# Three of four heads turned in blocks through HBM, cached values loaded in one contiguous transfer

## The chip, the cores and the metric

The kernel runs on one core of a Trainium2 chip. Its five engines are TensorE (PE; PEld are its weight loads), VectorE (DVE), ScalarE (ACT), GpSimd (POOL) and SyncE (SP), which here issues nearly all DMAs. The metric is the device time of one execution in microseconds.

## The reference, cut to what matters

For 8 sequences of 128 tokens and width 512 the reference computes a layer with LoRA and a first attention (32 heads of 16), adds the result to x, then a second attention with grouped heads over a paged cache, then a feed-forward layer with low-rank experts, and adds that too. The change touches the second attention alone:

```python
q = _rope(_rmsnorm(q, q_norm_w), pos)          # 32 query heads of 128
k = _rope(_rmsnorm(k, k_norm_w), pos)          # 8 key heads, 128 new keys
kc = k_cache[block_table].reshape(bsz, L, HK, D)   # 16 pages of 32 keys: L = 512
k_all = jnp.concatenate([kc, k], axis=1)       # 640 keys
v_all = jnp.concatenate([vc, v], axis=1)
scores = jnp.einsum('bqhd,bkhd->bhqk', q, k_all) * SCALE
probs = jax.nn.softmax(jnp.where(valid, scores, -1e+30), axis=-1)
o = jnp.einsum('bhqk,bkhd->bqhd', probs, v_all)
return jnp.einsum('bse,de->bsd', o, Wo)        # summed over all heads
```

## The kernel before, in words

The first stage (`phase1`) ends at about 250 us of the profile. Beside its own work it gathers the cached pages of each sequence into the HBM tensor `kv_of_batch` (`gather_four`, line 86). The second stage (`phase2`) runs 64 items: for each of 8 key heads g the 8 sequences b. An item has four query heads (`REP`). All products are done to nearly full f32 precision by splitting each factor into a rounded high part (`_h`, made on ACT) and a remainder (`_l`, made on DVE or POOL), and three matmuls.

The probabilities of a head come out with the queries on the partitions (`pf`, 128 x 640) and are needed with the keys on the partitions. Two ways do this. Heads in `BY_PE` are turned by five PE transposes into PSUM (line 1317), copied by ACT (`high`, line 1486) and subtracted by DVE (`low`, line 1610). Heads in `BY_DMA` are turned by DVE in blocks of 32 x 32 into `blk` (line 1604), stored to HBM (`blocks_away`, line 1217) and loaded back by four DMAs that put the blocks into their places in `moved` (`blocks_back`, line 1226); ACT then makes the high part (`high_moved`, line 1492) and POOL the remainder (`low_moved`, line 1745). Heads 0 and 1 go by DMA, heads 2 and 3 by PE. `ck` and `cv` hold the cached keys and values of an item.

The order of each engine's work is written out by hand: each engine has a function `slot(m, one, two, last)`, called once per item. In the slot of item m the scores of its heads 1 to 3 are computed, the values of item `last` are multiplied, item `one`, which follows, is made ready and its head 0 started, and queries and keys of item `two` are projected. Engines run their lists strictly in order and meet by semaphores. PE's scores of one head wait for DVE's `minima` (line 1590) of the head before, since both use the same two PSUM banks. ACT's `exponent` (line 1480) follows the minima. In the slots with b equal to 5 and 6 the next head's projection weights are split, on POOL by `q_weights` (line 1697) and `kv_weights` (line 1703); in those with b equal to 0 and 1 the output weights are. `rope_queries` is line 1722, `rope_keys` lines 1728 and 1731, `rms` 1715 and 1717, the remainders of cached keys and values lines 1739 and 1735. SP's `key_rows` (line 1204) waits until POOL has read the keys before (`kcl_sb`), `value_rows` (line 1210) until it has read the values before (`vcl_sb`). The third stage, from about 1252 us, is the feed-forward layer.

## Time and profile before

| | us |
|---|---|
| median of 3 runs | 1304.53 (1304.43 to 1305.79) |
| profiled execution, its own time | 1303.22 |
| its span in the profile | 1301.4 |
| PE busy | 1252.7 |
| DVE busy | 984.4 |
| ACT busy | 835.0 |
| POOL busy | 830.8 |
| DMA queue q1, share of 16 engines' span | 51.0% |

The span is what the profile covers; the execution's own time is 1.8 us longer. Busy times count work, not waiting, and PE's contains overlapping instructions once. Times in the rows below are from the span's start.

### The profile page before, as it was taken

Reading aid. Unit: us, or ns where it says so; the run is one execution under the profiler, and the core shown is the slowest. Engines: PE = TensorE matmul, PEld = TensorE weight load, DVE = VectorE, ACT = ScalarE, POOL = GpSimd, SP = SyncE. Lnnn points to the kernel's source line nnn. Section 1 sums busy time; section 2 is a strip of 40 time slices with the busy share of each in tenths; the row PEclk is TensorE's granted clock in tenths of the full one; section 3 lists DMA queues with packets and bytes.
Section 4 is the critical chain, followed back from the end, with each engine's and each line's share of the span. In section 5 each row is a group of like instructions: output and inputs, shape, how many; then the busy total and the mean of one; then the engine's idle time right before and its main releaser. Section 6 shows DMA issues by size and latency. Waiting matters only on the chain. (4 is left out here: it accounts for less than half of the span.)

```text
span 1301.4 us, 26180 instructions
## 1 busy us (share of the span) xinstructions
PE 1252.7 (96%) x7464; PEld 1067.8 (82%) x7464; DVE 984.4 (76%) x2380; ACT 835.0 (64%) x2501; POOL 830.8 (64%) x783
## 2 busy tenths in 40 slices
PE   5899998799999999999999999999999999999988
PEld 4666765588888888888888888888888888888878
DVE  3577757478878878888788788868888888888866
ACT  2677777466676666666766666666667666666731
POOL 1457557476767676668765876577667756775731
PEclk9899998899999999999999999999999999999999
DMA  8555553445555545555555555545555555555541
GB/s 288 214 200 205 203 211 130 111 117 139 137 139 141 140 133 149 131 140 141 151 130 141 138 140 128 144 126 139 131 140 143 137 142 142 135 138 137 137 130 66
DMA packets 288561, 191.48 MB, mean 147 GB/s; under 512 B 151201, under 2 KB 256674, under 8 KB 287266
## 3 DMA queue, kind: packets, MB, share of 16 engines
q1 hardware_dynamic: 287408, 189.64, 51.0%
q8 instruction: 61, 1.00, 0.3%
q14 instruction: 82, 0.67, 0.2%
q10 hardware_dynamic: 1010, 0.17, 0.1%
HBM read 143.60 MB, written 79.69 MB: 172 GB/s over the span
## 5 line engine op out<-in xcount | busy, mean ns | idle before, releaser
L1745 POOL TENSOR_TENSOR b_p_l<-b_moved,b_p_h 128x640 fp32r<-128x640 f32 x128 | 200.9, 1570 | 167.4 <-PE ps L1341 86.5
L1480 ACT ACTIVATE b_pf<-b_sm,b_mn 128x640 f32<-128x640 f32 x256 | 212.2, 829 | 128.0 <-DVE b_mn L1590 127.9
L1590 DVE CUSTOM_DVE_ANT_0 b_sm<-ps,mask_row,b_rstd 128x640 f32<-128x640 f32 x256 | 224.9, 878 | 51.8 <-PE ps L1267 46.5
L1492 ACT ACTIVATE b_p_h<-b_moved 128x640 fp32r<-128x640 f32 x128 | 94.6, 739 | 163.5 <-DMA b_moved<-blocks_of_probs 162.0
L1626 DVE SCALAR_TENSOR_TENSOR b_hacc<-ps,b_ri,b_hacc 128x512 f32<-128x512 f32 x248 | 182.4, 736 | 4.3 <-PE ps L1267 4.0
L1265 PE MATMUL ps<-b_w_h,x1t_h 128*128 128x512 f32 (+1 forms) x512 | 179.3, 350 | 0.1
L1265 PE MATMUL ps<-b_kt_h,b_qt_h 128*128 128x320 f32 x512 | 168.9, 330 | 6.0 <-DVE b_mn L1590 5.7
L1266 PE MATMUL ps<-b_w_l,x1t_h 128*128 128x512 f32 (+1 forms) x512 | 173.8, 340 | 0.0
L1267 PE MATMUL ps<-b_w_h,x1t_l 128*128 128x512 f32 (+1 forms) x512 | 173.6, 339 | 0.0
L1267 PE MATMUL ps<-b_kt_h,b_qt_l 128*128 128x320 f32 x512 | 158.9, 310 | 0.0
L1266 PE MATMUL ps<-b_kt_l,b_qt_h 128*128 128x320 f32 x512 | 158.7, 310 | 0.0
L1610 DVE TENSOR_TENSOR b_p_l<-ps,b_p_h 128x640 fp32r<-128x640 f32 x128 | 104.8, 819 | 41.1 <-ACT b_p_h L1486 41.1
L1604 DVE STREAM_TRANSPOSE b_blk<-b_pf 128x640 f32<-128x640 f32 x128 | 107.7, 842 | 35.2 <-ACT b_pf L1480 34.3
L1735 POOL TENSOR_TENSOR b_v_l<-b_cv,b_v_h 128x512 fp32r<-128x512 f32 x64 | 82.9, 1295 | 58.8 <-ACT b_v_h L1462 58.8
L711 POOL TENSOR_TENSOR a_pr<-a_pr,a_ri 128x512 f32<-128x512 f32 x64 | 68.4, 1078 | 74.8 <-DVE a_ri L586 74.8
L1265 PEld LDWEIGHTS ps<-b_kt_h,b_qt_h 128*128 128x128 f32 x512 | 96.8, 189 | 14.5 <-DVE b_mn L1590 8.1
L1267 PEld LDWEIGHTS ps<-b_w_h,x1t_l 128*128 128x128 f32 x512 | 96.7, 189 | 12.0
L431 ACT ACTIVATE a_pr<-a_sm,a_mn 128x128 f32<-128x128 f32 x256 | 99.0, 396 | 10.9 <-PE ps L304 10.6
L1265 PEld LDWEIGHTS ps<-b_w_h,x1t_h 128*128 128x128 f32 x512 | 97.0, 189 | 9.7 <-issue 0.8
L1265 PE MATMUL ps<-b_wo_h,b_o_h 128*128 128x512 f32 x256 | 101.6, 397 | 3.1 <-DVE b_o_l L1614 2.0
L1266 PEld LDWEIGHTS ps<-b_w_l,x1t_h 128*128 128x128 f32 x512 | 97.1, 190 | 8.7
L1333 PE MATMUL ps<-b_p_h,b_v_l 128*128 128x512 f32 x256 | 102.4, 400 | 0.0
(170 smaller groups left out, 3344.6 us busy)
## 6 DMA issues: line engine op xcount, KB each, us to landing
blocks_of_probs<-b_blk SPq DMA_DIRECT2D x128, 320.0 KB, 2.5
b_moved<-blocks_of_probs SPq DMA_DIRECT2D x512, 80.0 KB, 2.0
kv_of_batch<-in_kv SPq DMA_DIRECT2D x128, 256.0 KB
b_ck<-kv_of_batch SPq DMA_DIRECT2D x64, 256.0 KB, 4.0
b_cv<-kv_of_batch SPq DMA_DIRECT2D x256, 64.0 KB, 1.9
raw<-in_w SPq DMA_DIRECT2D x32, 384.0 KB, 3.2
raw<-in_wo SPq DMA_DIRECT2D x32, 256.0 KB, 2.8
a_xt<-in_xt SPq DMA_DIRECT2D x8, 256.0 KB, 5.6
```

The source lines that it names most:

```text
L431: op = act.activation(pr[:, c % 4, j], sm[:, c % 2, j], ACT.Exp, bias=mn[:, h:h + 1], scale=-1.0, accum_out=rs[:, h:h + 1])
L1265: pe.matmul(out, lhs[0], rhs[0], start=start, stop=False)
L1266: pe.matmul(out, lhs[0], rhs[1], start=False, stop=False)
L1267: return pe.matmul(out, lhs[1], rhs[0], start=False, stop=stop)
L1333: mm = pe.matmul(ps[:, OT, :], l, p_h[:, i], start=False, stop=False)
L1480: act.activation(pf[:, h % 2], sm[:, h % 2], ACT.Exp, bias=mn[:, m.b % 2, h:h + 1], scale=-1.0, accum_out=rs[:, m.b % 2, h:h + 1]).then_in ...
L1492: act.activation(blocks_of(p_h[:, :, h * P:(h + 1) * P]), moved[:, d].rearrange("p (a t j) -> p a t j", a=LT, j=QUAD), ACT.Copy).then_inc( ...
L1590: dve.tensor_tensor_reduce(sm[:, h % 2], score_row, mask_row[:, m.b], rstd[:, m.b % 4, h:h + 1], -MASKED, ALU.add, ALU.min, mn[:, m.b % 2, ...
L1604: dve.transpose(by_quadrant(blk[:, d]), by_tile(pf[:, h % 2])).then_inc(blk_sb, 1)
L1610: dve.tensor_tensor(p_l[:, :, cols], turned_row, p_h[:, :, cols], ALU.subtract).then_inc(pl_sb, 1)
L1626: dve.scalar_tensor_tensor(out=hacc[:, m.b], in0=ps[:, OUT[h], :], scalar=share, in1=hacc[:, m.b], op0=ALU.mult, op1=ALU.add).then_inc(h_s ...
L1745: pool.tensor_tensor(blocks_of(p_l[:, :, h * P:(h + 1) * P]), moved[:, d].rearrange("p (a t j) -> p a t j", a=LT, j=QUAD), blocks_of(p_h[: ...
```

## The change

Head 2 moves from `BY_PE` to `BY_DMA`. `blk` and `moved` keep two rooms, so heads 0 and 2 share one, and new waits order them. Head 2's copy on ACT and its subtraction on POOL are placed in the following slot. ACT's copy of head 0 moves behind the exponent of head 3. `kv_of_batch` holds keys and values apart, and the values of an item are loaded by one DMA that gives each partition four keys in a row (2 KB). Partition p of tile t thus holds key 4p + t instead of 128t + p, and so the probabilities of cached keys are read with a step of four elements, by DVE's block transposes (which become two instructions, since the 128 new keys keep their order) and by PE's transposes.

```diff
...
 LAST = B - 1
-BY_DMA = (0, 1)
-BY_PE = (2, 3)
+BY_DMA = (0, 1, 2)
+BY_PE = (3,)
+ROOMS = 2
 QUAD = 32
...
         n = first + k
-        sp.dma_start(kv_dram[n // NPP, :, n % NPP], t["kv"][bass.ds(four[k], 1)].rearrange("a g n -> (a g) n")).then_inc(gathered, 16)
+        page = t["kv"][bass.ds(four[k], 1)].rearrange("a g (k n) -> (a g) k n", k=2)
+        sp.dma_start(kv_dram[n // NPP, :, :, n % NPP], page).then_inc(gathered, 16)
 
...
         hacc = sb("hacc", [P, B, D])
-        blk = sb("blk", [P, len(BY_DMA), NK])
-        moved = sb("moved", [P, len(BY_DMA), NK])
+        blk = sb("blk", [P, ROOMS, NK])
+        moved = sb("moved", [P, ROOMS, NK])
 
...
 
+        def last_in_room(d):
+            return max(e for e in range(len(BY_DMA)) if e % ROOMS == d % ROOMS)
+
         def by_quadrant(ap):
...
         def by_tile(ap):
-            return ap.rearrange("p (t c j) -> p c t j", c=LT, j=QUAD)
+            return ap.rearrange("p (c j t) -> p c t j", c=LT, j=QUAD)
+
+        def by_rows(ap):
+            return ap.rearrange("p (c j) -> p c j", j=QUAD)
 
...
                 wait(sp, kcl_sb, m.n)
-                keys = kv_dram[m.b, m.g, :, 0:HD * PSIZE].rearrange("j (d s) -> d j s", d=HD)
+                keys = kv_dram[m.b, m.g, 0].rearrange("j (d s) -> d j s", d=HD)
                 sp.dma_start(ck[:].rearrange("p (j s) -> p j s", s=PSIZE), keys).then_inc(ck_in, 16)
...
                 wait(sp, vcl_sb, m.n)
-                for q in range(LT):
-                    rows_of = kv_dram[m.b, m.g, :, HD * PSIZE:].rearrange("(t q) (s d) -> q s t d", q=LT, d=HD)[q]
-                    sp.dma_start(cv[q * PSIZE:(q + 1) * PSIZE], rows_of).then_inc(cv_in, 16)
+                rows_of = kv_dram[m.b, m.g, 1].rearrange("j (p n) -> (j p) n", n=LT * HD)
+                sp.dma_start(cv[:].rearrange("p t d -> p (t d)"), rows_of).then_inc(cv_in, 16)
 
...
                 wait(sp, moved_in[d], 16 * LT * m.n)
-                sp.dma_start(blocks_dram[d], blk[:, d]).then_inc(blk_out[d], 16)
+                sp.dma_start(blocks_dram[d], blk[:, d % ROOMS]).then_inc(blk_out[d], 16)
 
...
                 sp.wait_ge(blk_out[d], 16 * (m.n + 1))
-                wait(sp, ml_sb, len(BY_DMA) * (m.n - 1) + d + 1)
+                wait(sp, ml_sb, len(BY_DMA) * m.n + d + 1 - ROOMS if d >= ROOMS else len(BY_DMA) * (m.n - 1) + last_in_room(d) + 1)
                 for c in range(LT):
                     rows_of = blocks_dram[d].rearrange("(a i) (c n) -> c i a n", a=LT, c=LT)[c]
-                    sp.dma_start(moved[c * QUAD:(c + 1) * QUAD, d].rearrange("p (a n) -> p a n", a=LT), rows_of).then_inc(moved_in[d], 16)
+                    sp.dma_start(moved[c * QUAD:(c + 1) * QUAD, d % ROOMS].rearrange("p (a n) -> p a n", a=LT), rows_of).then_inc(moved_in[d], 16)
 
...
                 blocks_back(m, 1)
+                blocks_away(m, 2)
+                blocks_back(m, 2)
                 if two:
...
                 for i in range(NT):
-                    mm = pe.transpose(turned_row[:, i], pf[:, h % 2, i * P:(i + 1) * P], ident[:])
+                    keys = pf[:, h % 2, L:] if i == LT else pf[:, h % 2, i:L:LT]
+                    mm = pe.transpose(turned_row[:, i], keys, ident[:])
                 mm.then_inc(pt_ps, 1)
...
                     turn_new(one)
-                turn_probs(m, 2)
                 if two:
...
             def cache_values(m):
-                act.wait_ge(cv_in, 16 * LT * (m.n + 1))
+                act.wait_ge(cv_in, 16 * (m.n + 1))
                 wait(act, pv_ps, m.n - 1)
...
                 wait(act, pvh_ps, m.n)
-                act.activation(blocks_of(p_h[:, :, h * P:(h + 1) * P]), moved[:, d].rearrange("p (a t j) -> p a t j", a=LT, j=QUAD),
+                act.activation(blocks_of(p_h[:, :, h * P:(h + 1) * P]), moved[:, d % ROOMS].rearrange("p (a t j) -> p a t j", a=LT, j=QUAD),
                                ACT.Copy).then_inc(mh_sb, 1)
...
                     high(last, 3)
+                    high_moved(last, 2)
                 exponent(m, 1)
...
                     kv_weights(m.g + 1)
-                high_moved(m, 0)
                 if last:
...
                 exponent(m, 3)
-                high(m, 2)
+                high_moved(m, 0)
                 if one:
...
             high(end, 3)
+            high_moved(end, 2)
             h_out(act, 2)
...
                 dve.wait_ge(exp_sb, REP * m.n + h + 1)
-                wait(dve, blk_out[d], 16 * m.n)
-                dve.transpose(by_quadrant(blk[:, d]), by_tile(pf[:, h % 2])).then_inc(blk_sb, 1)
+                wait(dve, blk_out[d - ROOMS], 16 * (m.n + 1)) if d >= ROOMS else wait(dve, blk_out[last_in_room(d)], 16 * m.n)
+                blocks = by_quadrant(blk[:, d % ROOMS])
+                dve.transpose(blocks[:, :, 0:LT], by_tile(pf[:, h % 2, 0:L]))
+                dve.transpose(blocks[:, :, LT], by_rows(pf[:, h % 2, L:])).then_inc(blk_sb, 1)
 
...
                 minima(m, 3)
+                turn_blocks(m, 2)
                 if last:
...
                     invert(last)
-                low(m, 2)
                 if one:
...
                 wait(pool, pv_ps, m.n)
-                pool.tensor_tensor(blocks_of(p_l[:, :, h * P:(h + 1) * P]), moved[:, d].rearrange("p (a t j) -> p a t j", a=LT, j=QUAD),
+                pool.tensor_tensor(blocks_of(p_l[:, :, h * P:(h + 1) * P]), moved[:, d % ROOMS].rearrange("p (a t j) -> p a t j", a=LT, j=QUAD),
                                    blocks_of(p_h[:, :, h * P:(h + 1) * P]), ALU.subtract).then_inc(ml_sb, 1)
...
                     rms(one)
+                if last:
+                    low_moved(last, 2)
+                if one:
                     rope_keys(one)
...
             slots(pool, slot)
+            low_moved(end, 2)
             pool_ffn(pool)
...
     x1_dram = nc.dram_tensor("x1", [B, S, D], F32).ap()
-    kv_dram = nc.dram_tensor("kv_of_batch", [B, G, NPP, 2 * HD * PSIZE], F32).ap()
+    kv_dram = nc.dram_tensor("kv_of_batch", [B, G, 2, NPP, HD * PSIZE], F32).ap()
     with ExitStack() as ctx:
```

The first place is POOL, from the queries' rope in the slot with b = 5 to the cached keys' remainder in that with b = 6. `b_rstd` is rms, `b_ka` the keys' rope, `b_w_l` weights, `b_kt_l` the cached keys' remainder. Before:

```order
L1722 TENSOR_TENSOR b_ra<-b_ra,b_rb 128x512 [waits b_qab_sb]
L1697 TENSOR_TENSOR b_w_l<-raw,b_w_h 128x512 [waits b_wqh_sb] x2
L1715 TENSOR_SCALAR b_rstd<-b_ss 128x5 [waits b_ksq_sb,b_exp_sb]
L1717 TENSOR_TENSOR b_rstd<-b_rstd,half 128x5 [waits b_ms_sb]
L1728 TENSOR_TENSOR b_ka<-b_ka,b_kb 128x128 [waits b_rstd_sb,b_kab_sb]
L1731 TENSOR_SCALAR b_ka<-b_ka,b_rstd 128x128 [waits b_kab2_sb]
L1697 TENSOR_TENSOR b_w_l<-raw,b_w_h 128x512 [waits b_wqh_sb] x2
L1739 TENSOR_TENSOR b_kt_l<-b_ck,b_kt_h 128x512 [waits b_kch_sb]
```

and now:

```order
L1734 TENSOR_TENSOR b_ra<-b_ra,b_rb 128x512 [waits b_qab_sb]
L1709 TENSOR_TENSOR b_w_l<-raw,b_w_h 128x512 [waits b_wqh_sb] x2
L1727 TENSOR_SCALAR b_rstd<-b_ss 128x5 [waits b_ksq_sb,b_exp_sb]
L1729 TENSOR_TENSOR b_rstd<-b_rstd,half 128x5 [waits b_ms_sb]
L1757 TENSOR_TENSOR b_p_l<-b_moved,b_p_h 128x4x5x32 [waits b_pv_ps,b_mh_sb]
L1740 TENSOR_TENSOR b_ka<-b_ka,b_kb 128x128 [waits b_rstd_sb,b_kab_sb]
L1743 TENSOR_SCALAR b_ka<-b_ka,b_rstd 128x128 [waits b_kab2_sb]
L1709 TENSOR_TENSOR b_w_l<-raw,b_w_h 128x512 [waits b_wqh_sb] x2
L1751 TENSOR_TENSOR b_kt_l<-b_ck,b_kt_h 128x512 [waits b_kch_sb]
```

One more subtraction of moved blocks, that of head 2 of the item before, stands between rms and the keys' rope; after it the order is as before.

The second place is SP in an ordinary slot, from the first block store to the values. `blocks_of_probs<-b_blk` is a store, `b_moved<-blocks_of_probs` the loads, `b_ck` keys and `b_cv` values. Before:

```order
L1217 DMA blocks_of_probs<-b_blk 128x640 [waits b_moved_in0,b_blk_sb]
L1226 DMA b_moved<-blocks_of_probs 32x4x160 [waits b_ml_sb,b_blk_out0]
L1226 DMA b_moved<-blocks_of_probs 32x4x160 x3
L1217 DMA blocks_of_probs<-b_blk 128x640 [waits b_moved_in1,b_blk_sb]
L1204 DMA b_ck<-kv_of_batch 128x16x32 [waits b_kcl_sb]
L1226 DMA b_moved<-blocks_of_probs 32x4x160 [waits b_ml_sb,b_blk_out1]
L1226 DMA b_moved<-blocks_of_probs 32x4x160 x3
L1210 DMA b_cv<-kv_of_batch 32x4x128 [waits b_vcl_sb]
L1210 DMA b_cv<-kv_of_batch 32x4x128 x3
```

and now:

```order
L1224 DMA blocks_of_probs<-b_blk 128x640 [waits b_moved_in0,b_blk_sb]
L1233 DMA b_moved<-blocks_of_probs 32x4x160 [waits b_ml_sb,b_blk_out0]
L1233 DMA b_moved<-blocks_of_probs 32x4x160 x3
L1224 DMA blocks_of_probs<-b_blk 128x640 [waits b_moved_in1,b_blk_sb]
L1212 DMA b_ck<-kv_of_batch 128x16x32 [waits b_kcl_sb]
L1233 DMA b_moved<-blocks_of_probs 32x4x160 [waits b_ml_sb,b_blk_out1]
L1233 DMA b_moved<-blocks_of_probs 32x4x160 x3
L1224 DMA blocks_of_probs<-b_blk 128x640 [waits b_moved_in2,b_blk_sb]
L1233 DMA b_moved<-blocks_of_probs 32x4x160 [waits b_ml_sb,b_blk_out2]
L1233 DMA b_moved<-blocks_of_probs 32x4x160 x3
L1217 DMA b_cv<-kv_of_batch 128x512 [waits b_vcl_sb]
```

A store and four loads for head 2 stand ahead of the values, which are one DMA instead of four.

## Rows read from the trace of the kernel before

**Rows 1.** The page's first part: busy us (share of the span) xinstructions.

```profile
PE 1252.7 (96%) x7464; PEld 1067.8 (82%) x7464; DVE 984.4 (76%) x2380; ACT 835.0 (64%) x2501; POOL 830.8 (64%) x783
```

**Rows 2.** Busy by stretch: us, PE, PEld, DVE, ACT, POOL; clock, DMA share, GB/s.

```profile
250.00:1252.00 1002.00, 992.62 (x5667) 871.13 (x5667) 799.39 (x1579) 669.12 (x1834) 688.93 (x639) 0.99 0.52 137
673.20:688.90 15.70, 15.70 (x94) 13.84 (x92) 12.72 (x26) 9.91 (x29) 9.07 (x9) 1.00 0.58 148
720.20:735.90 15.70, 15.70 (x94) 13.84 (x91) 12.59 (x25) 10.46 (x23) 14.59 (x13) 1.00 0.44 121
735.90:751.50 15.60, 14.96 (x83) 12.63 (x82) 11.44 (x23) 11.15 (x37) 10.96 (x11) 1.00 0.56 147
```

**Rows 3.** PE in order of time: start, us, line, op, tiles, count.

```profile
681.37 0.71 PE L1317 MATMUL ps<-ident,b_pf 128*128 128x128 f32 x5
681.83 0.48 PE L1265 MATMUL ps<-b_w_h,x1t_h 128*128 128x512 f32 x1
682.15 0.39 PE L1266 MATMUL ps<-b_w_l,x1t_h 128*128 128x512 f32 x1
682.38 0.39 PE L1267 MATMUL ps<-b_w_h,x1t_l 128*128 128x512 f32 x1
```

**Rows 4.** DVE in order of time, the same slot.

```profile
676.17 0.28 DVE L1571 TENSOR_TENSOR b_ka<-ps,cw 128x128 f32<-128x128 f32 x1
676.37 0.28 DVE L1573 TENSOR_TENSOR b_kb<-ps,sw 128x128 f32<-128x128 f32 x1
...
678.10 0.84 DVE L1604 STREAM_TRANSPOSE b_blk<-b_pf 128x640 f32<-128x640 f32 x1
...
683.50 0.83 DVE L1610 TENSOR_TENSOR b_p_l<-ps,b_p_h 128x640 fp32r<-128x640 f32 x1 [0.63 <-ACT b_p_h L1486]
```

**Rows 5.** Groups, 440:1240: busy us, mean ns | idle before.

```profile
L1492 ACT ACTIVATE b_p_h<-b_moved 128x640 fp32r<-128x640 f32 x102 | 75.4, 739 | 128.4 <-DMA b_moved<-blocks_of_probs 126.9 <-PE ps L1333 1.4
...
L1745 POOL TENSOR_TENSOR b_p_l<-b_moved,b_p_h 128x640 fp32r<-128x640 f32 x102 | 160.2, 1570 | 124.8 <-PE ps L1341 70.6 <-ACT b_p_h L1492 54.1
```

**Rows 6.** DMA issues: count, KB each, us from issue to landing.

```profile
blocks_of_probs<-b_blk SPq DMA_DIRECT2D x128, 320.0 KB, 2.5
b_moved<-blocks_of_probs SPq DMA_DIRECT2D x512, 80.0 KB, 2.0
```

**Rows 7.** SP in order of time, an ordinary slot and the seventh.

```profile
681.93 1.91 SPq L1226 DMA_DIRECT2D b_moved<-blocks_of_probs  x4
...
730.14 0.38 SPq L1204 DMA_DIRECT2D b_ck<-kv_of_batch  x1
730.62 2.59 SPq L1226 DMA_DIRECT2D b_moved<-blocks_of_probs  x4
```

**Rows 8.** ACT in order of time, two slots [idle before].

```profile
675.43 0.83 ACT L1480 ACTIVATE b_pf<-b_sm,b_mn 128x640 f32<-128x640 f32 x1 [0.91 <-DVE b_mn L1590]
...
689.48 0.70 ACT L1486 ACTIVATE b_p_h<-ps 128x640 fp32r<-128x640 f32 x1
...
735.30 0.74 ACT L1492 ACTIVATE b_p_h<-b_moved 128x640 fp32r<-128x640 f32 x1 [4.18 <-DMA b_moved<-blocks_of_probs]
```

**Rows 9.** POOL in order of time, first and last of ten instructions.

```profile
719.60 1.30 POOL L1722 TENSOR_TENSOR b_ra<-b_ra,b_rb 128x512 f32<-128x512 f32 x1
...
728.81 1.30 POOL L1739 TENSOR_TENSOR b_kt_l<-b_ck,b_kt_h 128x512 fp32r<-128x512 f32 x1
```

**Rows 10.** DVE's block transposes: an ordinary one (689.20), three late ones.

```profile
360.41 0.84 DVE L1604 STREAM_TRANSPOSE b_blk<-b_pf 128x640 f32<-128x640 f32 x1 [1.56 <-ACT b_pf L1480]
...
689.20 0.84 DVE L1604 STREAM_TRANSPOSE b_blk<-b_pf 128x640 f32<-128x640 f32 x1 [0.33 <-ACT b_pf L1480]
...
737.91 0.85 DVE L1604 STREAM_TRANSPOSE b_blk<-b_pf 128x640 f32<-128x640 f32 x1 [2.05 <-ACT b_pf L1480]
...
1118.12 0.85 DVE L1604 STREAM_TRANSPOSE b_blk<-b_pf 128x640 f32<-128x640 f32 x1 [1.24 <-ACT b_pf L1480]
```

**Rows 11.** PE in order of time, after the seventh slot.

```profile
738.99 0.66 PE L1293 MATMUL ps<-ident,b_ra 128*128 128x128 f32 x4 [0.64 <-POOL b_ra L1722]
```

## The prediction

> **What bounds the kernel now.** I read the page's busy times, then the busy times by stretch, then each engine in order of time. [Rows 1] show TensorE (PE) busy for 96% of the span. [Rows 2] cut the second stage, 250 to 1252 us, out of it: 992.6 of 1002.0 us are PE time, at a granted clock of 0.99. The stage has 64 items, so an item takes 1002.0 / 64 = 15.66 us, and the slots of one head (eight items) show PE 15.70 of 15.70 us while DVE has 12.7, ACT 10 to 11 and POOL 9.07 in an ordinary slot but 14.59 in the seventh, where the next head's weights are split. Only after that seventh slot does PE lose time: 14.96 of 15.60 us. So in seven slots of eight a matmul taken away is time taken away, as long as nothing else becomes late; around the seventh slot something else ends last.
>
> **What the change takes from PE.** One of two groups of five turns per item goes (head 2). [Rows 3] show the group start at 681.37 us and the next matmul at 681.83 us, 0.46 us; that matmul's successor comes 0.32 us later where the following pairs are 0.23 us apart, so 0.09 us more belong to the group. 64 x 0.55 = 35.2 us.
>
> **What it adds, off PE.** On DVE, the remainder of head 2 (0.83 us at 683.50, with 0.63 us of waiting for ACT ahead of it) goes and a third block transpose comes (0.84 us at 678.10) [rows 4]. Each block transpose is now two instructions, 512 and 128 elements wide. Small instructions of 128 elements stand 0.20 us apart [rows 4]; the small one can cost from nearly nothing beyond its share of the work (0.20 less a fifth of 0.84, so 0.03 us) to the whole 0.20 us. I take 0.1 us, 0.3 per item. DVE then has 12.7 - 0.83 + 0.84 + 0.3 = 13.0 of 15.1 us. The new transpose follows the minima of head 3, which themselves follow the exponent of head 2 by their order, so it waits for nothing. ACT exchanges one copy of 640 columns for another, of 739 ns [rows 5]: nothing, with some 5 us of idle time per item. POOL gets a third 1570 ns subtraction [rows 5]: 9.1 + 1.6 = 10.7 of 15.1 us, free in an ordinary slot.
>
> On the queue, SP gets one store and four loads more and three loads of values fewer. Four loads take SP 1.91 us (at 681.93), and landings take 2.5 and 2.0 us [rows 6, 7]. For head 2: the last load of head 1 is issued by 683.84 us, then 2.5 us until the store has landed, 1.9 us of issuing and 2.0 us of landing: 690.2 us. The copy that wants it stands behind ACT's copy of head 3, which ends at 690.18 us [rows 8], 0.55 us earlier once the slot is shorter. So it is some 0.6 us late, and what waits behind it on ACT is the exponent of head 1, which already stood idle 0.91 us for DVE [rows 8] and so hides it; if landings grow by 1 us, this cover is gone, and the exponent delays the minima of head 3 on DVE. The values' load moves behind the loads of head 2, which wait for POOL's subtraction of head 0. It is wanted only in the next slot (a slot of 15 us against some 5 us of delay), so nothing. DMA queues are busy for 0.52 of the stage [rows 2]; 640 KB more per item on some 2.1 MB make it 0.65 at most, less what 2 KB rows for the values save. The cache gather writes the same bytes in two pieces per row: nothing, under the first stage.
>
> **The seventh slot.** Here POOL works without a gap: the queries' rope, two weights, rms, the keys' rope, two weights and the cached keys' remainder run from 719.60 to 730.11 us, ten instructions [rows 9]. SP's load of keys waits for that last one and starts at 730.14; the loads of head 1's blocks stand behind it, at 730.62 [rows 7]. ACT stood idle 4.18 us for them and took them at 735.30 [rows 8]; the exponent behind them was late, and so was DVE's block transpose at 737.91, with 2.05 us of idle time where an ordinary slot has 0.33 [rows 10]. The minima that free the score banks for PE follow it. POOL's own last piece, the queries' rope, held PE for 0.64 us at 738.99 [rows 11]. The late block transpose stands at the end of seven heads (the first at 360.41, the last at 1118.12). The change puts head 2's subtraction, 1.57 us, into this chain, ahead of the keys' rope. The chain begins in the sixth slot (where POOL takes up 719.60) and ends in the eighth, so the two groups of turns that PE saves inside it, 1.1 us, are not gained either. Its price is between 0 (if its slack were as large as it) and 7 x (1.57 + 1.1) = 18.7 us; since PE waited here already, I take all of it.
>
> **The sum.** 1303.2 (the profiled execution) - 35.2 + 18.7 = 1286.7 us. The median of the runs is 1.3 us above that execution: 1288.
>
> **A price that no row shows: strided reads.** DVE and PE now read the probabilities of cached keys with a step of four elements, 16 bytes; every read of that tile so far was contiguous. Below, it is nothing, and a gain is excluded, since the same elements are read. Above, I double the strided part: on DVE 0.84 x 512/640 = 0.67 us per transpose, 2.0 us per item; on PE four of five turns at 0.46 / 5 = 0.093 us, 0.37 us per item. I take nothing, which is what [rows 3, 4] show for the contiguous form, and keep the other end as a rival.
> The Trainium skill speaks against it: SBUF — State Buffer, Specifications (TRN2), says that SBUF delivers lines of 16 bytes and that full bandwidth needs at least two reads in each. By that rule each read here would open a new line, and the time would be that of rival 1 below; by [rows 3, 4] it would be the sum above. No run so far shows it.
>
> **The rivals.**
> 1. *Strided reads are charged.* DVE gets 13.0 + 2.0 = 15.0 us of work per item plus the waits that its order can't lose, 0.33 us for the exponent [rows 10] and about as much for the scores: 15.7 to 15.8 us; DVE then paces, from an extra cost of about 0.45 us per transpose on. With the seventh slots' chain (7 x 1.6 us, and 7 x 1 us as the transposes in it grow), 1303 + 64 x 0.12 + 18 + 1.3 = 1330. Nothing in the trace speaks for or against it, since no instruction of this stage reads such a step. That is slower than before.
>    The page named above, of the Trainium skill, is what makes me hold this for possible.
> 2. *POOL's chain has room.* If the subtraction slips in where POOL would wait anyway, all 35 us are gained: 1303.2 - 35.2 + 1.3 = 1269. Against it: ten instructions in 10.5 us of [rows 9].
> 3. *The third head comes back late.* If the extra transfers lengthen the landings by 1 us, ACT's in-order copy of head 2 holds the exponent of head 1 for some 0.6 us per item more than it idled, and the loads of head 0 on SP wait for POOL's subtraction of head 2. Half of that reaching PE gives 0.3 x 56 = 17 us: 1305. For it: ACT's 4.18 us for such loads in [rows 8]; against: the 0.91 us of idle time there.
> 4. *Only one of the two engines is charged* for the strides: PE alone, at half of its 0.37 us per item, 64 x 0.2 = 13 us more than the forecast: 1301.
>
> **Chances.** Forecast 0.42, rival 1 0.27, rival 2 0.12, rival 3 0.12, rival 4 0.07. A measurement of this kernel tells 0.2% (2.6 us) from no change. Faster: nearly all of the forecast and rival 2, about half of rivals 3 and 4, together 0.60; within 0.2%: 0.07; slower: rival 1 and the rest, 0.33. The forecast's own range is 1276 to 1297: 12 us less if two thirds of the chain's price are hidden, 9 more if half as much again comes on top. For 8 in 10 it reaches from 1268 down at rival 2 to 1328, just short of rival 1's middle.
>
> **What the profile after will show.** Right: 320 turns on PE, slots of 15.1 us in the first five of a head, block transposes of about 0.7 and 0.2 us, a PE wait of some 2 to 4 us after each seventh slot, released by DVE's minima. Wrong: block transposes of 1.2 us or more, a pitch of turns above 0.1 us, ordinary slots with PE waiting for minima (rival 1); or ACT's copy of head 2 idle for over 1.5 us in ordinary slots (rival 3).

## The result: 4.7% slower

The changed kernel takes **1363.51 us** (median, 1362.68 to 1364.49), the kernel before beside it 1304.48 (1297.11 to 1305.79). The ratio is 1.0469, interval 1.0441 to 1.0498. The forecast of 1288 us was wrong in sign, and the time lies outside its own range (1276 to 1297) and above the wider one (1268 to 1328). The profiled execution has a span of 1360.9 us, 59.5 us more than that of before (1301.4).

The page's first part and the busy times by stretch of the kernel after answer to [rows 1, 2]:

```profile
PE 1251.9 (92%) x7144; PEld 1043.4 (77%) x7144; DVE 1057.9 (78%) x2572; ACT 828.5 (61%) x2501; POOL 925.0 (68%) x847
```
```profile
250.00:1310.00 1060.00, 992.98 (x5347) 848.14 (x5345) 870.11 (x1765) 661.73 (x1834) 779.25 (x699) 0.98 0.61 168
```

TensorE has 320 matmuls fewer. The stage is 58 us longer, and by these rows the growth is idle time of TensorE: 67 us now, 9 before. But its busy time should have fallen by some 31 us and didn't, so part of it is slower work; that is taken up below. No other engine is near full. The slots show where the time sits. I measure a slot from one group of turns of head 3 to the next, in TensorE's order of time; this is the second full head of each kernel (us; the last column but one is the next head's first slot):

```
slot of sequence      2      3      4      5      6      7      8      1      sum
before              15.66  15.66  15.66  15.66  15.66  15.66  16.19  15.66  125.8
after               15.80  19.04  15.18  15.17  15.55  17.14  19.15  15.17  132.2
```

An undisturbed slot did become shorter, 15.17 instead of 15.66 us, as forecast (15.1). In most heads two or three of eight are undisturbed; the others are not. Over the stage the mean slot of after is (1313.35 - 259.63) / 63 = 16.73 us.

A slot in which TensorE stands idle long can cost twice. Here is the eighth slot of that head and four of its microseconds (us, PE, PEld, DVE, ACT, POOL; granted clock, DMA share, GB/s):

```profile
494.29:513.44 19.15, 17.17 (x88) 14.43 (x86) 13.45 (x29) 11.81 (x38) 13.21 (x12) 0.91 0.60 166
497.00:498.00 1.00, 0.33 (x2) 0.00 (x0) 0.17 (x1) 1.00 (x5) 1.00 (x2) 1.00 0.64 172
498.00:499.00 1.00, 0.11 (x1) 0.11 (x2) 1.00 (x2) 0.82 (x3) 0.91 (x2) 1.00 0.83 168
501.00:502.00 1.00, 1.00 (x5) 0.81 (x4) 1.00 (x3) 0.86 (x2) 1.00 (x2) 0.50 0.41 161
502.00:503.00 1.00, 1.00 (x4) 0.81 (x3) 1.00 (x3) 0.27 (x1) 0.83 (x2) 0.50 0.03 8
```

From 497 to 500 us TensorE was busy for 1.02 us (0.58 in the third microsecond). From 501 to 504 its granted clock was 0.50, that is 1.2 instead of 2.4 GHz, and from 505 on full again. So this slot has 2.0 us of idle time and 2.0 us more of busy time than an undisturbed one. Ten of the 63 slots of after show a mean clock of 0.91 or 0.92; before has one, the slot of 19.65 us in its fifth head. From the eight whole ones (busy 137.7 us, where the other long slots have 15.4 to 16.0 each) I estimate that the lower clock makes 12 to 16 of the 59 us. It is a consequence of the waiting, and adds to it.

The queue at fault, as the experiments below bear out, belongs to none of the busy engines: it is that of SyncE (SP), which issues all transfers in order and waits in between. Here is its order of time in after for one slot (start, us of issuing), answering to [rows 7]. L1224 is the store of a head's blocks, L1233 the four loads back, L1212 keys, L1217 values:

```profile
813.38 1.73 SPq L1233 DMA_DIRECT2D b_moved<-blocks_of_probs  x4
815.15 0.43 SPq L1217 DMA_DIRECT2D b_cv<-kv_of_batch  x1
816.56 0.44 SPq L1224 DMA_DIRECT2D blocks_of_probs<-b_blk  x1
820.52 1.74 SPq L1233 DMA_DIRECT2D b_moved<-blocks_of_probs  x4
822.36 0.38 SPq L1224 DMA_DIRECT2D blocks_of_probs<-b_blk  x1
822.94 0.38 SPq L1212 DMA_DIRECT2D b_ck<-kv_of_batch  x1
825.06 1.74 SPq L1233 DMA_DIRECT2D b_moved<-blocks_of_probs  x4
826.90 0.38 SPq L1224 DMA_DIRECT2D blocks_of_probs<-b_blk  x1
829.23 1.73 SPq L1233 DMA_DIRECT2D b_moved<-blocks_of_probs  x4
```

Read it as three trips (heads 0, 1, 2): store, wait until it has landed, four loads. From head 2's loads at 813.38 to the next at 829.23 it is 15.85 us, more than the 15.17 that TensorE needs. SP's own waits between 440 and 1250 us, summed, say what stands behind whom (us, times, longest); L63 is the helper that waits, here for GpSimd's subtractions. After, and then two lines of before:

```profile
SPq L1233 <- DMA blocks_of_probs<-b_blk: 186.7, 116, 4.1
SPq L63 <- POOL b_p_l L1757: 151.4, 66, 4.0
SPq L1224 <- DVE b_blk L1616: 29.6, 43, 1.6
SPq L1212 <- POOL b_kt_l L1751: 17.4, 13, 2.7
```
```profile
SPq L1226 <- DMA blocks_of_probs<-b_blk: 177.5, 97, 3.1
SPq L1217 <- DVE b_blk L1604: 115.0, 87, 6.7
```

SP waits for blocks from VectorE only 29.6 us in 810, where it was 115.0 before: now it is nearly always late. ScalarE, in order of time, is where the lateness enters the computation, answering to [rows 8]; L1501 is a copy of a head that came back, L1489 an exponent:

```profile
812.62 0.74 ACT L1501 ACTIVATE b_p_h<-b_moved 128x640 fp32r<-128x640 f32 x1 [3.13 <-DMA b_moved<-blocks_of_probs]
...
814.26 0.85 ACT L1489 ACTIVATE b_pf<-b_sm,b_mn 128x640 f32<-128x640 f32 x1
...
818.05 0.74 ACT L1501 ACTIVATE b_p_h<-b_moved 128x640 fp32r<-128x640 f32 x1 [1.83 <-DMA b_moved<-blocks_of_probs]
818.69 0.81 ACT L1489 ACTIVATE b_pf<-b_sm,b_mn 128x640 f32<-128x640 f32 x1
```

Each exponent starts with no wait of its own, right behind the copies: what held it is the copy ahead of it. The exponent feeds VectorE's block transpose, whose blocks SP stores: a ring of two in-order queues. GpSimd stands in a second ring: its subtraction of head 2 ended at 820.44 (818.86 + 1.58), and head 0's loads, which need the same room, start at 820.52:

```profile
818.86 1.58 POOL L1757 TENSOR_TENSOR b_p_l<-b_moved,b_p_h 128x640 fp32r<-128x640 f32 x1 [1.05 <-ACT b_p_h L1501]
```

TensorE itself names only the last link, VectorE's minima and GpSimd's rotary products (PE waits, 250 to 1310 us), as [rows 11] did:

```profile
PE ps L1274 <- DVE b_mn L1600: 31.7, 44, 2.4
PE ps L1302 <- POOL b_ra L1734: 26.4, 23, 2.8
PE ps L1342 <- ACT b_p_h L1501: 5.6, 8, 1.1
```

The two terms that the prediction left open, as groups of VectorE and TensorE's weight loads (count, busy us, mean ns), and the landings, answering to [rows 3, 4, 6]:

```profile
L1615 DVE STREAM_TRANSPOSE b_blk<-b_pf 128x512 f32<-128x512 f32 x192 | 214.1, 1115 | 109.2 <-ACT b_pf L1489 105.2 <-DMA blocks_of_probs<-b_blk 4.0
L1616 DVE STREAM_TRANSPOSE b_blk<-b_pf 128x128 f32<-128x128 f32 x192 | 52.3, 272 | 0.0
```
```profile
713.14 0.76 PE L1327 MATMUL ps<-ident,b_pf 128*128 128x128 f32 x5
713.66 0.39 PE L1274 MATMUL ps<-b_kt_h,b_qt_h 128*128 128x320 f32 x1
```
```profile
blocks_of_probs<-b_blk SPq DMA_DIRECT2D x192, 320.0 KB, 2.7
b_moved<-blocks_of_probs SPq DMA_DIRECT2D x768, 80.0 KB, 2.0
```

### The profile page after: what moved, and what is told of

It reads as the page before. It is cut to its first block and busy times, and to the rows that moved or that the text cites. A ratio compares the mean times of both kernels' runs of the same rounds, so it can differ in the third digit from the quotient of the medians.

```text
span 1360.9 us, 26051 instructions
## 1 busy us (share of the span) xinstructions
PE 1251.9 (92%) x7144; PEld 1043.4 (77%) x7144; DVE 1057.9 (78%) x2572; ACT 828.5 (61%) x2501; POOL 925.0 (68%) x847
## 5 line engine op out<-in xcount | busy, mean ns | idle before, releaser
L1757 POOL TENSOR_TENSOR b_p_l<-b_moved,b_p_h 128x640 fp32r<-128x640 f32 x192 | 301.7, 1571 | 262.6 <-ACT b_p_h L1501 262.1
L1615 DVE STREAM_TRANSPOSE b_blk<-b_pf 128x512 f32<-128x512 f32 x192 | 214.1, 1115 | 109.2 <-ACT b_pf L1489 105.2
L1501 ACT ACTIVATE b_p_h<-b_moved 128x640 fp32r<-128x640 f32 x192 | 141.7, 738 | 220.9 <-DMA b_moved<-blocks_of_probs 220.6
L1489 ACT ACTIVATE b_pf<-b_sm,b_mn 128x640 f32<-128x640 f32 x256 | 212.0, 828 | 51.8 <-DVE b_mn L1600 51.1
L1274 PE MATMUL ps<-b_kt_h,b_qt_h 128*128 128x320 f32 x512 | 171.9, 336 | 32.5 <-DVE b_mn L1600 31.7
L1507 ACT ACTIVATE b_o_h<-ps 128x512 fp32r<-128x512 f32 x64 | 38.3, 599 | 128.9 <-PE ps L1351 128.9
L1342 PE MATMUL ps<-b_p_h,b_v_h 128*128 128x512 f32 x256 | 108.3, 423 | 5.6 <-ACT b_p_h L1501 5.6
L1343 PE MATMUL ps<-b_p_h,b_v_l 128*128 128x512 f32 x256 | 107.3, 419 | 0.0
```

The costliest lines, as they stand in the source:

```text
L1274: pe.matmul(out, lhs[0], rhs[0], start=start, stop=False)
L1342: pe.matmul(ps[:, OT, :], h, p_h[:, i], start=i == 0, stop=False)
L1343: mm = pe.matmul(ps[:, OT, :], l, p_h[:, i], start=False, stop=False)
L1489: act.activation(pf[:, h % 2], sm[:, h % 2], ACT.Exp, bias=mn[:, m.b % 2, h:h + 1], scale=-1.0, accum_out=rs[:, m.b % 2, h:h + 1]).then_in ...
L1501: act.activation(blocks_of(p_h[:, :, h * P:(h + 1) * P]), moved[:, d % ROOMS].rearrange("p (a t j) -> p a t j", a=LT, j=QUAD), ACT.Copy).t ...
L1615: dve.transpose(blocks[:, :, 0:LT], by_tile(pf[:, h % 2, 0:L]))
```

## The experiments

Times are medians; runs of one group shared a chip and its runs of the kernel before (1306.18, 1304.88, 1305.62, 1303.31 and 1303.39 us in the order of the groups; 1303.67 for the last run, whose runs of before were its own).

### First group: which part, and which suspect

**Three heads alone** (values loaded as before, no strided reads):

```diff
-rows_of = kv_dram[m.b, m.g, 1].rearrange("j (p n) -> (j p) n", n=LT * HD)
-sp.dma_start(cv[:]...)
+for q in range(LT):
+    sp.dma_start(cv[q * PSIZE:(q + 1) * PSIZE], rows_of).then_inc(cv_in, 16)
...
-dve.transpose(blocks[:, :, 0:LT], ...)   # 512, step 4
-dve.transpose(blocks[:, :, LT], ...)     # 128
+dve.transpose(blocks, by_tile(pf[:, h % 2]))   # 640, contiguous
...
-keys = pf[:, h % 2, L:] if i == LT else pf[:, h % 2, i:L:LT]
+keys = pf[:, h % 2, i * P:(i + 1) * P]         # TensorE's turns
```


> Three heads by DMA as after, but values loaded as before (four DMAs, keys 128t + p), so that no read has a step of 16 bytes and each block transpose is one instruction. Theory A (DVE's strided transposes, 1115 ns for 512 columns where the 128-column one takes 272, set the pace): DVE loses 3 x 0.54 us per item and the time falls to 1285 to 1300. Theory B (SP's one queue, three store-landing-load trips in a row per item, sets the pace): three more DMAs on SP, so 1355 to 1375, about that of after.

Measured 1425.69 us (1423.99 to 1426.74), ratio 1.0900 [1.0862, 1.0939]: slower still by 62 us. So the strides are not the cause, and the value load was worth something after all: the four value loads take SP 2.02 us to issue where one takes 0.43. An extra 1.6 us of SP's time costs about 1 us a slot, and SP waits for blocks from VectorE 0.7 us in all (440 to 1250 us): SP paces. Part of the 62 us is again the clock: 21 slots are below 0.93, where after has ten. Undisturbed slots take 15.10 to 15.12 us, so all of the 0.55 us that the prediction wanted from TensorE is there once the reads are contiguous.

```profile
816.85 2.02 SPq L1218 DMA_DIRECT2D b_cv<-kv_of_batch  x4
```

**The value layout alone** (two heads by DMA, one value load, strided reads):

```diff
-BY_DMA = (0, 1, 2)
-BY_PE = (3,)
+BY_DMA = (0, 1)
+BY_PE = (2, 3)
```


> Two heads by DMA as before, with the new layout of values: one DMA of 2 KB rows, strided reads by DVE (two transposes) and by PE (ten turns). Theory A: DVE gets 2 x 0.54 us per item more and the time rises to 1325 or more. Theory B: SP's queue is shorter than before; only PE's turns, if they take longer, and the seventh slots show: 1300 to 1312.

Measured 1317.04 (1314.61 to 1325.84), ratio 1.0080 [1.0053, 1.0107]. Its undisturbed slots are 15.75 us against 15.66: two groups of strided turns, 0.05 us each by that, 0.06 by the order of time of after (0.52 us from 713.14 to 713.66, against 0.46 in [rows 3]). That makes 6 us; the rest stands in the eighth slots, 123.1 us for seven of them against 116.1 in before (its trace is of the longest of its seven runs, 1325.84 us). The two parts don't add: +11 and +120 alone, +59 together. The layout costs a little where TensorE paces and pays where SP does.

**A room for each head** in the tile that the loads fill:

```diff
-moved = sb("moved", [P, ROOMS, NK])
+moved = sb("moved", [P, len(BY_DMA), NK])
...
+wait(sp, ml_sb, len(BY_DMA) * (m.n - 1) + d + 1)   # each head waits for its own subtraction only
```


> After, with a room of its own in moved for each of the three heads (blk keeps two), so SP's loads of head 0 don't wait for POOL's subtraction of head 2, nor those of head 2 for head 0's. If the shared room is what holds SP (the profile names POOL for 161 us of SP's waits), 1335 to 1350; if it is the landings of the stores (198 us of SP's waits) or DVE, 1360 to 1365.

Measured 1362.52 (1355.4 to 1369.15), ratio 1.0414 [1.0355, 1.0473]: no gain that can be told from none. SP's wait for GpSimd is gone, but its wait for landings rose from 186.7 to 313.7 us. Cutting the ring through GpSimd only uncovers the other.

**No round trip for head 2** (its store and loads are left out, and its blocks are read where they lie, in a room of their own, so its probabilities stand in wrong places; with that the wait of head 0's loads for GpSimd's subtraction of head 2 goes too):

```diff
-blocks_away(m, 2)
-blocks_back(m, 2)
```


> After, without head 2's store and loads: ACT and POOL read head 2 straight from DVE's blocks, whose places are then wrong, all other work is as after. Theory B: SP's chain and 640 KB per item go, 1290 to 1310 (POOL's seventh slot and DVE's strides stay). Theory A: 1350 or more, since DVE's work is unchanged.

Measured 1317.43 (1316.29 to 1320.22), ratio 1.0086 [1.0050, 1.0122]: head 2's trip is 46 of the 59 us, the shared room included, which by itself was worth nothing in the run before. But with no trip at all the kernel is still 11 us slower than before, in slots at the heads' boundary (its eighth slots take 17.6 to 20.7 us).

### Second group: order, bytes, queue, stride

**Other loads into SP's wait** for head 2's store:

```diff
 blocks_away(m, 2)
-blocks_back(m, 2)
 if two: value_rows(two)
 ...                     # weight chunks
+blocks_back(m, 2)
```


> The changed kernel with only the order of SyncE's queue edited: the value load and the weight chunks of a slot are issued between head 2's store and its four loads back, where SyncE otherwise waits for the store to land. Same bytes, same instructions. Theory S (SyncE's one in-order queue sets the long slots: three times store, wait for the landing, four loads): these issues, 0.43 us for the values and 0.43 us for a chunk, leave the chain, up to 0.9 us of each long slot, and the next head 0's store no longer lands behind them; about 35 of the 64 slots are long, so 20 to 40 us come back: 1325 to 1345 us. Theory D (the 640 KB more of DMA traffic per item make every landing late): the traffic is the same, 1358 to 1368.

Measured 1383.44 (1381.31 to 1386.61), ratio 1.0596 [1.0570, 1.0623]: theory S, as I put it, missed by 40 us and in sign. SP's waiting for landings did fall (186.7 to 85.6 us), but the value load now waits for GpSimd ahead of head 2's loads (62.2 us), and ScalarE's waits for loads grew from 171.9 to 210.5 us. My reading is that what counts is when head 2 comes back, not how long SP waits.

**A quarter of head 2's bytes**, every issue and wait kept (three quarters of its rows are not moved):

```diff
+rows = slice(0, QUAD) if h == 2 else slice(0, P)
-sp.dma_start(blocks_dram[d], blk[:, d % ROOMS])
+sp.dma_start(blocks_dram[d, rows], blk[rows, d % ROOMS])
...
+if h == 2: room, rows_of = room[:, 0:1], rows_of[:, 0:1]   # each of the four loads
```


> The changed kernel with every DMA of head 2's trip kept in its place, but each moving only a quarter of its rows (32 of 128 partitions stored, one of four tiles loaded in each of the four loads), so three quarters of head 2's probabilities are not head 2's. Same instructions and same waits on SyncE, 480 KB less traffic per item. Theory S (SyncE's serial queue): the issues and the waits stay and only the landings get a little shorter; 1345 to 1362. Theory D (traffic): most of the trip's 46 us go, 1317 to 1330, as without the trip.

Measured 1342.68 (1333.78 to 1343.74), ratio 1.0271 [1.0226, 1.0316]: between both theories. 21 of the 46 us go with the bytes, 25 stay with the issues and waits. The store of 80 KB lands in 1.8 us, the one of 320 KB in 2.7, so a shorter landing alone could explain the 21.

**Head 2's trip on ScalarE's queue:**

```diff
 high_moved(m, 0)
+blocks_away(m, 2)      # act.dma_start
 ...
 high_moved(m, 1)
+blocks_back(m, 2)      # act.dma_start x4, waits for the landing
```


> The changed kernel with head 2's trip issued by ScalarE instead of SyncE: its store behind the copy of head 0's moved probabilities, its four loads behind the copy of head 1's. Same bytes. Theory S: SyncE is back at two trips per slot as before the change, ordinary slots stay at 15.17 us, and ScalarE (busy 662 of 1060 us) pays some 5 x 0.4 us an item out of its idle time: 1315 to 1335. Theory D: 1355 to 1368.

Measured 1439.96 (1435.89 to 1441.83), ratio 1.1024 [1.0994, 1.1055], the worst of all. SP got its slack (231.7 us of waiting for blocks), and TensorE's wait for minima rose to 71.9 us between 440 and 1250. ScalarE now waits itself for the landing and for the other heads' loads, ahead of every exponent: here a wait moved into a queue that computes costs more than one in SP's. The loads themselves were late too: from ScalarE's queue they landed in 3.3 us (median), from SP's in 2.2. In 23 slots the granted clock is below 0.93.

**Contiguous block transposes** (the keys stand in wrong places for the values):

```diff
-by_tile(pf[:, h % 2, 0:L])
+pf[:, h % 2, 0:L].rearrange("p (t c j) -> p c t j", c=LT, j=QUAD)
```


> The changed kernel with VectorE's 512-column transposes reading their columns in a row instead of every fourth one (the keys then stand in the wrong places for the values). TensorE's turns stay strided. The transpose should fall from 1115 ns to about 700 ns, worked out from the 128-column transpose (272 ns) and the 640-column one of the kernel before (842 ns). Theory S: SyncE hardly waits for VectorE's blocks (31 us in all), so the 1.25 us saved per item are worth little: 1350 to 1362. Theory V (the strided transposes are what holds the slots): 1320 to 1335.

Measured 1372.51 (1367.81 to 1379.92), ratio 1.0520 [1.0470, 1.0569], no faster than the changed kernel. The transpose fell from 1115 to 710 ns:

```profile
L1615 DVE STREAM_TRANSPOSE b_blk<-b_pf 128x512 f32<-128x512 f32 x192 | 136.4, 710 | 141.7 <-ACT b_pf L1489 141.6
```

The stride's price is 0.41 us an instruction, 1.2 us an item, and to save it buys nothing here: VectorE was waiting for ScalarE (105.2 us before these transposes) and waits longer now (141.6).

### Third group: the order on SP, and the key load

**Head 2's store ahead of head 1's loads**, shared rooms and then three:

```diff
-blocks_back(m, 1)
 blocks_away(m, 2)
+blocks_back(m, 1)
 blocks_back(m, 2)
...                      # in the second run: rooms as in the first group
```


> The changed kernel with one edit in SyncE's order: head 2's store is issued before head 1's four loads back instead of behind them, so that its landing (2.2 us) passes while those loads are issued (1.74 us). Same bytes, instructions and rooms. Theory L (a loop of latencies through SyncE: head 2's loads land, ScalarE copies, GpSimd subtracts, only then may head 0's loads of the next item go; 2.9 + 0.74 + 1.58 + 0.1 + 4.16 + 4.12 + 1.73 = about 15.9 us read from one long slot, against 15.17 us that TensorE needs): some 2 us leave the loop, it drops below 15.17, and the slots that are not the seventh or eighth fall to 15.2: 1325 to 1345. Theory D (traffic makes the landings late): no change, 1358 to 1368.

> The order of the run before, and a room of its own for each head in the tile that the loads fill. Theory L: both loops, that through ScalarE and GpSimd and SyncE's own of 15.9 us with three landings, are then cut, about what the kernel without the round trip takes: 1317 to 1335. If the shared room is the tighter loop this comes out 5 to 20 us below the order alone. Theory D: 1355 to 1368.

Measured 1375.10 (1372.56 to 1377.32), ratio 1.0549 [1.0521, 1.0577], and 1373.47 (1371.42 to 1375.72), ratio 1.0528 [1.0498, 1.0559]. Theory L, that one loop through SP is the whole cause, fell. With three rooms SP has slack now, as its waits show:

```profile
SPq L1224 <- DVE b_blk L1616: 253.0, 136, 3.8
SPq L1233 <- DMA blocks_of_probs<-b_blk: 92.6, 59, 2.3
SPq L1212 <- POOL b_kt_l L1751: 35.9, 27, 4.1
```

Yet slots are 15.9 us. Head 1's loads now wait for head 2's blocks, so they come later, and ScalarE's copy of head 1 holds the next exponent:

```profile
841.66 0.74 ACT L1501 ACTIVATE b_p_h<-b_moved 128x640 fp32r<-128x640 f32 x1 [2.83 <-DMA b_moved<-blocks_of_probs]
843.31 0.85 ACT L1489 ACTIVATE b_pf<-b_sm,b_mn 128x640 f32<-128x640 f32 x1
```

**The key load of the seventh slot behind head 1's loads**, with the edits of the run before, and in the kernel before:

```diff
-if two:
+if two and m.b != 6:
     key_rows(two)
 blocks_back(m, 1)
+if two and m.b == 6:
+    key_rows(two)
```


> The run before with one more edit: in the slot of the seventh sequence SyncE issues the key load behind head 1's loads. There the key load waits for GpSimd, which splits weights first, and head 1's loads are queued behind it (4.1 us late in the kernel without the round trip, where TensorE then stood still 3 us in the eighth slot). Theory P (that queueing makes the eighth slots of 17.5 to 20 us): seven or eight of them fall by 1.5 to 3 us, 10 to 22 us below the run before. Rival: GpSimd's own time in the seventh slot (16.2 us of work) does it, and the order on SyncE changes less than 4 us.

> The kernel before with the same edit of the seventh slot alone: the key load behind head 1's loads. Its eighth slots are 15.7 to 19.7 us against 15.66. Theory P: 2 to 6 us faster, 1299 to 1303. Rival (GpSimd's own time): within 2 us of 1304.5.

Measured 1351.05 (1348.40 to 1354.29), ratio 1.0367 [1.0334, 1.0400], 22 us less than the run before; and **1295.04** (1294.26 to 1295.54), ratio **0.9929** [0.9904, 0.9954], for the kernel before. Theory P held in both, and the second is faster than forecast (1299 to 1303). In its trace the seven eighth slots take 109.9 us, in that of before 116.1; the rest of the difference isn't placed by these two traces. In [rows 7] the key load starts at 730.14, when GpSimd has freed its tile, with head 1's loads behind it; now the loads go first, and the key load doesn't hold them:

```profile
725.07 1.73 SPq L1226 DMA_DIRECT2D b_moved<-blocks_of_probs  x4
726.84 0.44 SPq L1204 DMA_DIRECT2D b_ck<-kv_of_batch  x1
```

### Fourth group: ScalarE's queue

**Head 1's copy behind the next exponent:**

```diff
 # ScalarE
-high_moved(m, 1)
 ...
     exponent(one, 0)
+high_moved(m, 1)
 # GpSimd
-low_moved(m, 1)
 if two: rope_queries(two)
+low_moved(m, 1)
```


> The changed kernel with the copy of head 1's moved probabilities behind the next item's first exponent on ScalarE (it stood ahead of it), and head 1's subtraction behind the rotary products on GpSimd. Theory Q (the trip's lateness reaches TensorE through ScalarE's in-order queue: the copy waits up to 3.2 us for the loads, and the first exponent, then head 0's blocks, wait behind it): exponents no longer wait, ordinary slots fall to 15.2 and the eighth ones with them: 1310 to 1340. Rival (SyncE's own chain paces, whatever ScalarE does): 1355 to 1366, and the copy only waits elsewhere.

Measured 1380.02 (1370.23 to 1383.10), ratio 1.0575 [1.0516, 1.0634]. Theory Q alone missed: SP's waits for blocks fell to 2.3 us, so exponents earlier by themselves only queue more work before SP.

**The key-load edit in the changed kernel:** the diff above, nothing else.


> The changed kernel with only the key load of the seventh slot issued behind head 1's loads, as in the run that brought the kernel before to 1295. Theory P: the eighth slots (17.8 to 20.6 us) fall to some 16.5, eight times about 3 us: 1336 to 1345. Rival: less than 5 us, 1358 or more.

Measured 1364.59 (1360.06 to 1369.78), ratio 1.0473 [1.0426, 1.0520]: nothing, where theory P expected 20 us. Seven eighth slots did fall, from 137.1 to 122.6 us in sum, but the other slots grew by nearly as much: where SP is late all the time, what one slot gains there another loses.

**Both, with three rooms:**


> Both edits of the two runs before, and a room for each head in the tile that the loads fill. Theory Q with P: only the strided turns, GpSimd's 16.2 us in the seventh slots and single late landings stay: 1280 to 1300, under the kernel before. Rival (SyncE's chain of three landings paces): 1325 to 1345.

Measured 1359.69 (1352.91 to 1365.24), ratio 1.0446 [1.0401, 1.0491]. Missed, but the clearest view of the rival. SP waits for landings and for little else:

```profile
SPq L1233 <- DMA blocks_of_probs<-b_blk: 357.9, 145, 4.3
SPq L1212 <- POOL b_kt_l L1753: 12.5, 13, 2.9
SPq L1224 <- DVE b_blk L1618: 2.0, 5, 0.8
```

That is 7.3 us of landings in a mean slot of 16.5 us ((1304.87 - 263.01) / 63); most of the rest is issuing: twelve loads, three stores, keys, values, a chunk, 7.6 us by the times shown. The 1.6 us left over are gaps that I can't name.

**No round trip, with the key-load edit** (head 2's probabilities in wrong places):


> The kernel without head 2's round trip (its store and loads left out, so its probabilities stand in the wrong places) with the key-load edit of the seventh slot. It was 1317.4. With P its eighth slots (17.6 to 20.7) fall to about 16.3, some 2.5 us seven times: 1296 to 1304. If GpSimd's own time is behind them, 1312 to 1318.

Measured 1296.88 (1293.67 to 1299.25), ratio 0.9947 [0.9932, 0.9963]: as theory P had it, 20.5 us below the run without the edit. Its eighth slots took between 17.6 and 20.7 us, and now take 16.3. Five of them had a granted clock of 0.91 or 0.92, now none has, so part of the gain is the clock's.

### Fifth group: both queues at once

**The overlap on SP and the late copy together** (three rooms, key load, order of the third group, copies of the fourth):


> Rooms, key load and late copy as in the run at 1359.7, and head 2's store issued ahead of head 1's loads as in the run at 1351.1: what neither had alone. Theory S+Q (two queues in a ring: SyncE's three landings and issues, 16 us or more, pace when ScalarE doesn't wait; when SyncE has slack, as in the run at 1351, head 1's later loads hold ScalarE's first exponent): with one landing covered SyncE needs about 14.5 us, nothing stands behind the late copy, and ordinary slots come to 15.2 us: 1290 to 1315. Rival (traffic D: DMA engines busy .63 make it slow in whatever order): 1345 to 1360.

Measured **1294.35** (1292.94 to 1297.75), ratio **0.9931** [0.9899, 0.9962]. This is the full computation of the changed kernel, and it is faster than the kernel before and the changed one. Without the late copy it is 1351.05, without the overlap 1359.69; in the changed kernel each edit by itself had cost 10 to 17 us, and where both are there the second gives back 57 to 65. Its stage moves the bytes of after in less time, at a DMA share of 0.65 instead of 0.61, and nothing suffers; TensorE's granted clock is 1.00, with one slot below 0.99 (windows, then SP's waits from 440 to 1250 us):

```profile
250.00:1242.00 992.00, 962.75 (x5334) 836.06 (x5335) 873.31 (x1767) 657.05 (x1830) 780.45 (x701) 1.00 0.65 180
```
```profile
SPq L1233 <- DMA blocks_of_probs<-b_blk: 140.2, 93, 3.8
SPq L1224 <- DVE b_blk L1618: 119.7, 112, 3.7
SPq L1212 <- POOL b_kt_l L1753: 76.1, 50, 3.8
```

SP now waits for its suppliers, as a queue that doesn't pace should. The same head of the stage, slots as in the first table (us):

```
slot of sequence                   2      3      4      5      6      7      8      1      sum
orders mended                    16.68  15.18  15.17  15.17  15.18  17.64  15.18  15.16  125.4
third group, with key-load edit  17.00  16.20  16.10  15.98  15.86  17.45  16.33  15.55  130.5
```

Six of eight are at 15.17. The two others, +1.5 and +2.5 us, belong to GpSimd's weight pieces, and eat the 0.49 us that each slot gained (8 x 0.49 = 3.9). So the full gain of the change, with its queues in order, is about that of the key-load edit in the kernel before: 1294.35 against 1295.04, the same within their ranges.

**GpSimd's weight pieces behind head 2's subtraction:**

```diff
 low_moved(last, 2)
+if m.b == 1: out_weights(m.g, 0); out_weights(m.g, 1)
+if m.b == 6: q_weights(m.g + 1, range(2))
...
 ...
-if m.b == 0: out_weights(m.g, 0); out_weights(m.g, 1)
-if m.b == 5: q_weights(m.g + 1, range(2))
```


> The version at 1294.35 with GpSimd's weight pieces that stood at the end of two slots (two output-weight pieces of the first sequence, two query-weight pieces of the sixth) issued in the following slot, behind the subtraction of head 2. TensorE waited for that subtraction 13 times, 16.6 us. Theory: the order is at fault; 1.3 to 1.5 us come back in each of the two slots of a group, 1275 to 1285. Rival: GpSimd's load in the slot stays (about 16 us of work in 15.17), and TensorE waits for the weights instead: 1290 to 1300.

Measured 1295.21 (1293.04 to 1296.75), ratio 0.9936 [0.9916, 0.9957]: no gain; the rival held. The wait of TensorE (250 to 1250 us) only changes its name, in the version before this edit and with it:

```profile
PE ps L1353 <- POOL b_p_l L1759: 19.1, 15, 1.3
```
```profile
PE ps L1309 <- POOL b_ka L1745: 18.9, 15, 1.3
```

So it isn't the order at this place. GpSimd's load is left as the cause (busy 15.76 us in the seventh slot of the second head, more than the 15.17 us of an undisturbed slot, and 14.80 in the second); no run took work from it.

## Why the prediction was wrong, point by point

- **What TensorE saves** was right: 0.55 us a slot with contiguous reads (15.66 to 15.11), as forecast; 0.49 with the strided turns, which is 31 us in all if every slot is undisturbed, of 35.2 forecast.
- **What hides beside other work** on VectorE, ScalarE and GpSimd was right for ordinary slots: with the orders mended they stay at 15.17 us with all three transposes, copies and subtractions in them.
- **The step that failed** is the overlap of head 2's trip: "For head 2: the last load of head 1 is issued by 683.84 us, then 2.5 us until the store has landed, 1.9 us of issuing and 2.0 us of landing: 690.2 us", and from it "So it is some 0.6 us late, and what waits behind it on ACT is the exponent of head 1, which already stood idle 0.91 us". It followed one trip from a start time taken out of the trace of before, and asked only for that copy. It never summed SP's queue round the slot. Summed, in the slot shown: from store to loads 3.96 us for head 0 (816.56 to 820.52), 2.70 for head 1 and 2.33 for head 2, three times 1.74 for the loads, 0.43 for the values: 9.0 + 5.2 + 0.4 = 14.6 us, and 0.98 more before head 0's store, 0.9 of it a wait for VectorE's blocks, of 15.85. In a slot with a weight chunk ahead of head 0's store, store to loads takes 3.8 us in the mean (39 trips, 440 to 1250 us) and 2.8 behind loads (91 trips): 9.3 + 5.2 + 0.9 = 15.4 us, against 15.17. (The key load hides in a landing; some of these times are waits for GpSimd.) Transfers hardly grew slower (medians 2.7 and 2.0 us against 2.5 and 2.0); the time is queueing. Shown: 46 us go with the trip, and 57 to 65 come back by the second of two reorderings, with no byte less.
- **The clock** was no term of the prediction. Where TensorE stood idle long, its granted clock fell to 0.50 for some microseconds, in ten slots against one: by my estimate 12 to 16 us of the 59.
- **Rival 3** named the right place (ScalarE's in-order copies) and the wrong size, 17 us where the trip costs 46, because it took the growth of the landings as its cause and half of it as hidden. Its second clause, head 0's loads behind GpSimd's subtraction of head 2, was a real ring (151.4 us of SP's waiting), but not the tightest: a room for each head alone gained nothing.
- **"The values' load ... so nothing"** was wrong where SP paces: one load in place of four, with its strided reads, is worth 62 us there. It was the change's best part, hidden by its worst.
- **Strided reads at nothing:** wrong for the instruction, nearly right for the kernel. They cost 0.41 us a transpose, just under the 0.45 us from which rival 1 let VectorE pace, and the split in two costs 0.14 more (710 + 272 against 842 ns), where 0.1 was forecast; the run with contiguous reads is no faster, and with the orders mended both hide in slots of 15.17 us. That this extra cost stayed just under the bound was luck, since nothing in the rows spoke for or against it. On TensorE they cost 0.06 us a slot, some 4 us in all. By the rule of the Trainium skill that the prediction cited (SBUF — State Buffer, Specifications (TRN2)) such reads run below full bandwidth. The trace agrees in direction, 1115 against 710 ns; the page gives no size for a transpose.
- **The seventh slot, 18.7 us:** 17.4 us where nothing else disturbs it (7 x 2.48, from 17.65 - 15.17). TensorE waits there for GpSimd, as the prediction had it. But the eighth slot's loss, which the prediction read off [rows 7, 8] and booked to GpSimd, was SP's key load standing ahead of head 1's loads. One edit in SP's order takes it out, in the kernel before and in the one with the orders mended. A second loss, 1.5 us in each head's second slot (about 12 us), was not foreseen.
- **The DMA share** of "0.65 at most" doesn't follow from its own numbers, which give 0.52 x 2.74 / 2.1 = 0.68; it came to 0.61, and to 0.65 with the orders mended.

**What stays open.** Whether the three rooms, or the key-load edit, are needed once the orders are mended wasn't run, and with the two orders as they were, three rooms and the key-load edit together weren't either; so the 69 us between 1363.51 and 1294.35 belong to the four edits together. Nor is it settled how the 21 us of the quarter-size trip divide between a shorter landing and less contention.

## What to carry to other kernels

Treat the queue that issues transfers as an engine: sum its issues and the waits that it sits through in order, round one slot, and compare with the slot. If that sum is near the pace of the busiest engine, one more trip is not hidden, whatever the DMA share says. Add that a matmul engine left idle may come back at a lower clock: look at the granted clock of the slots that grew. Where two in-order queues feed each other, mending either alone can be worth nothing or less; try both before a theory is dropped. And a load that waits for a busy engine should not stand ahead of one that is ready.
